# Rolling the thirty middle images of a four-layer kernel into a hardware loop of three images

## The chip, the cores and the metric

The kernel runs on one core of a Trainium2 chip. Its time is the device time of one execution, in microseconds (us). The kernel before takes 14134.04 us, the median of three runs (14127.32 to 14146.60). The profile comes from one execution, which took 14127.32 us; its recorded span is 14125.5 us, so 1.8 us lie outside the span.

The engines are TensorE (PE for matmuls, PEld for weight loads), VectorE (DVE), ScalarE (ACT), GpSimd (POOL), and SyncE (SP), which here issues all DMA transfers. Each engine has a sequencer that reads the engine's instructions in order. Some instructions are the sequencer's alone: a semaphore wait, a register operation, a branch. They are not counted as busy time of the engine. The profile marks the sequencer with a q (DVEq, POOLq).

## The reference: what is computed

Thirty-two images of 128 channels by 32x32 pixels pass four residual layers, each on a group-normalised input:

```python
x = x + _L0_conv_ref(_gn(x), ...)   # 3x3 convolution
x = x + _L1_conv_ref(_gn(x), ...)   # four-direction state-space scan over 1024 pixels
x = x + _L2_conv_ref(_gn(x), ...)   # gated row and column means, with two short scans
x = x + _L3_conv_ref(_gn(x), ...)   # four-qubit circuit per pixel
```

Layer 1 takes nearly all of the time. For each of 4 directions, 256 inner channels and 16 states it runs a recurrence over the 1024 pixels:

```python
dA = jnp.exp(dt_t[..., None] * A)
h = dA * h + (dt_t * u_t)[..., None] * B_t[:, None, :]
y = jnp.einsum('bdn,bn->bd', h, C_t)
```

## The kernel before

**Units.** A unit is one state n of one half (128) of the inner channels in one direction: 4 x 2 x 16 = 128 units per image, each a tile of 128 partitions by 1024 pixels. Per unit, four engines work in turn:

- ACT makes the decay exp(dt * A) (L1164) and raises `decay_ready`.
- The input dt * u * B is made in one of three ways, which the table `KINDS` chooses. In a D unit (70 per image) PE spreads the row B over the partitions into a PSUM slot (`spread_b`, raises `b_ready`), and DVE multiplies it in place by `du` (L1446, raises `input_ready`). In a P unit (52 per image) POOL multiplies `du` by a row that a DMA has broadcast (L954, raises `pool_input`). In a Z unit (6 per image) PE and ACT make it (`z_turned`).
- DVE runs the recurrence as one scan (L1460, raises `scan_done`).
- POOL multiplies the scans of two units by their C rows (L971, one 128x2048 product per pair, 64 per image, raises `prod_ready`), and PE adds the products up in PSUM (`y_acc`, L1487, raises `sum_done`).

The scans live in a ring of 8 unit buffers (`RING`), the C rows in 4 buffers, the broadcast B rows in 4.

**Side steps.** Everything else (layers 0, 2 and 3, the convolution and projections of layer 1, for this image and the next) is cut into small steps that a planner places between the units of each engine's program. Its result is a fixed order, the same for all middle images. `hold` writes the waits of a side step, `side` counts its completion.

**Semaphores and the image number.** No semaphore is ever reset. Every wait is for a count that has grown since the start of the program: unit u of image s waits for `scan_done >= s * UNITS + u + 1`, side steps for a base that grows by a fixed number per image (`bases`). In the DVE program a scan waits like this, in this order:

```python
dve.wait_ge(input_ready, s * N_D + number("D", u) + 1)
...
dve.wait_ge(decay_ready, s * UNITS + u + 1)
```

and a product on POOL like this:

```python
pool.wait_ge(c_in[k % CB_BUFS], 16 * (s * (PAIRS // CB_BUFS) + k // CB_BUFS) + 16)
pool.wait_ge(scan_done, s * UNITS + u + 1)
```

**The image loop.** `each_image` calls an engine's `image` function once per image at build time: "first", thirty times "mid", "last". So s is a plain number everywhere, every wait is for a constant, and each engine's program is one straight line of instructions for all 32 images.

An instruction carries one wait of its own. Where an operation waits for two semaphores, the builder puts one wait on the operation and the other on a separate wait instruction of the sequencer ahead of it. The profile calls that one EVENT_SEMAPHORE, and the chain of waits shows it as DVEq or POOLq.

Of the kernel before, what the change touches and what calls it, by code (L numbers as in the profile page):

```python
# [616 lines left out]
def four_layers(nc, images, x_in, keep, once, small, dtw, conv_wt, preb_row, qw, out):  # L617
# [36 lines left out]
    with ExitStack() as ctx:  # L654
# [91 lines left out]
        turns, turns_whole = q_sb[:, 48:96], scratch[0:1, 3408:3408 + 48]  # L746
# [34 lines left out]

        def each_image(eng, body):

            for s in range(images):
                body("first" if s == 0 else "last" if s == images - 1 else "mid", s)

        NONE = dict.fromkeys("PADG", 0)

# [27 lines left out]
        def _(sp):  # L816
# [48 lines left out]
            def image(kind, s):  # L865
# [26 lines left out]
                if kind != "last":  # L892
                    store_rows(0, base, of[("dt_cb_rows", 0, 1)])
                    for k in range(CB_BUFS):
                        load_pair(k, s + 1)

            each_image(sp, image)
            sp.wait_ge(*done(finish_base, finish_n[("result", 1)]))
            sp.dma_start(out[images - 1], x_old[:, :]).then_inc(out_stored, 16)
# [4 lines left out]
        def _(pool):  # L904
# [33 lines left out]
            def image(kind, s):  # L938
# [33 lines left out]
                side_steps(END["G"])  # L972

            each_image(pool, image)
            for _, name, e, _, after in finish:
                if e == "G":
# [5 lines left out]
        def _(act):  # L982
# [153 lines left out]
            def image(kind, s):  # L1136
# [34 lines left out]
                want(HOME)  # L1171

            each_image(act, image)
            for _, name, e, bank, after in finish:
                if e == "A":
# [619 lines left out]
```

## Time and profile before

| | |
|---|---|
| median of three runs | 14134.04 us |
| profiled execution, its span | 14127.32 us, 14125.5 us |
| instructions recorded | 172711 |
| POOL, DVE, PE, ACT busy share of the span | 94%, 92%, 89%, 74% |
| TensorE clock granted, mean of the run | 0.945 |
| DMA, mean | 222 GB/s |

The run is even. The 64 products of a middle image end about 433.5 us after those of the image before, all through the program, so one middle image stands for thirty. A busy share is an average; two engines above 90% that wait for each other leave the question open which of them sets the pace where. That is read from the waits and from the chain of waits, which follows the work that ended last back in time, at each step to what released it.

### The profile page before, as it was taken

Reading aid. Unit: us, or ns where it says so; the run is one execution under the profiler, and the core shown is the slowest. Engines: PE = TensorE matmul, PEld = TensorE weight load, DVE = VectorE, ACT = ScalarE, POOL = GpSimd, SP = SyncE. Lnnn points to the kernel's source line nnn. Section 1 sums busy time; section 2 is a strip of 40 time slices with the busy share of each in tenths; the row PEclk is TensorE's granted clock in tenths of the full one; section 3 lists DMA queues with packets and bytes.
Section 4 is the critical chain, followed back from the end, with each engine's and each line's share of the span. In section 5 each row is a group of like instructions: output and inputs, shape, how many; then the busy total and the mean of one; then the engine's idle time right before and its main releaser. Section 6 shows DMA issues by size and latency. Waiting matters only on the chain.

```text
span 14125.5 us, 172711 instructions
## 1 busy us (share of the span) xinstructions
PE 12502.9 (89%) x64412; PEld 8000.4 (57%) x64412; DVE 12955.6 (92%) x8813; ACT 10492.8 (74%) x14525; POOL 13337.0 (94%) x4106
## 2 busy tenths in 40 slices
PE   7889989899888898888988888988889989889886
PEld 4555555555555555555555555555555555555554
DVE  7999999999999999999999999999999999999986
ACT  5777777777777777777777777777777777777764
POOL 7999999999999999999999999999999999999985
PEclk8999999999999999999999999999999999999997
DMA  5665556655556655566555665555655556656653
GB/s 195 231 227 223 223 221 227 234 223 223 223 223 235 225 221 225 221 230 231 223 223 223 226 233 223 221 225 224 233 225 225 222 220 229 232 223 225 226 206 120
DMA packets 563751, 3131.63 MB, mean 222 GB/s; under 512 B 63826, under 2 KB 63834, under 8 KB 300642
## 3 DMA queue, kind: packets, MB, share of 16 engines
q1 hardware_dynamic: 562914, 3120.59, 58.6%
q8 instruction: 510, 8.36, 0.2%
q14 instruction: 327, 2.68, 0.1%
HBM read 3057.42 MB, written 46.14 MB: 220 GB/s over the span
## 4 chain that ended last, share of the span: by engine, by line
POOL 30%; issue 22%; PE 22%; DVE 20%; ACT 6%; POOLq 0%; DMA 0%; DVEq 0%; SPq 0%; ACTq 0%
POOL ring L971 20%; PE work L1472 12%; DVE ring L1460 11%; POOL ring L954 9%; DVE slot L1446 7%; PE y_acc L1487 6%; PE y_acc L1472 2%; PE slot L1472 2%; ACT L988 1%; ACT slot L1164 1%; ACT ring L1164 1%; ACT z_t L1067 1%; PE work L1487 1%; DVE du L1271 0%; PE slot L1487 0%
## 5 line engine op out<-in xcount | busy, mean ns | idle before, releaser
L971 POOL TENSOR_TENSOR ring<-ring,c_rows 128x2048 f32<-128x2048 f32 x2048 | 9284.2, 4540 | 435.6 <-DVE ring L1460 423.1
L1460 DVE TENSOR_TENSOR_SCAN ring<-ring,slot 128x1024 f32<-128x1024 f32 x2432 | 5544.3, 2284 | 162.5 <-PE slot L1487 68.4
L1487 PE MATMUL y_acc<-wk,ring 128*128 128x128 f32 x32768 | 4450.8, 284 | 515.1 <-POOL ring L971 447.4
L1487 PEld LDWEIGHTS y_acc<-wk,ring 128*128 128x128 f32 x32768 | 3941.3, 147 | 1565.5 <-POOL ring L971 671.3
L954 POOL TENSOR_TENSOR ring<-du,b_rows 128x1024 f32<-128x1024 f32 x1664 | 3938.4, 2368 | 63.3 <-DVE du L1271 54.2
L1460 DVE TENSOR_TENSOR_SCAN ring<-slot,ring 128x1024 f32<-128x1024 f32 x1664 | 3782.3, 2273 | 223.0 <-POOL ring L954 153.4
L1446 DVE TENSOR_TENSOR slot<-du,slot 128x1024 f32<-128x1024 f32 x2240 | 2713.8, 1212 | 138.4 <-PE slot L1472 134.2
L1164 ACT ACTIVATE slot<-dt,a_neg 128x1024 f32<-128x1024 f32 x1664 | 1854.2, 1114 | 1299.4 <-DVE ring L1460 1294.1
L1164 ACT ACTIVATE ring<-dt,a_neg 128x1024 f32<-128x1024 f32 x2432 | 2738.7, 1140 | 78.1 <-PE y_acc L1487 63.2
L1472 PE MATMUL work<-h_new,fused 128*128 128x512 f32 x4096 | 1935.9, 602 | 17.9 <-ACT yz L1076 8.8
L1472 PE MATMUL slot<-stack,sel 96*128 96x512 bf16 x4480 | 1407.4, 397 | 540.1 <-DVE ring L1460 503.9
L988 ACT ACT_TABLE_LOAD x1081 | 1386.9, 1283 | 19.1
L1472 PEld LDWEIGHTS slot<-stack,sel 96*128 96x128 bf16 x4480 | 343.3, 100 | 1491.1 <-DVE ring L1460 1038.2
L1472 PEld LDWEIGHTS work<-h_new,fused 128*128 128x128 f32 x4096 | 717.3, 190 | 740.4 <-issue 584.6
L1472 PE MATMUL work<-padded,wk 128*128 128x512 f32 (+1 forms) x1792 | 984.0, 652 | 55.8 <-ACT yz L1076 27.7
L1472 PE MATMUL work<-du,wk 128*128 128x512 f32 x1024 | 643.5, 715 | 76.2 <-ACT du L1055 73.8
L1047 ACT ACTIVATE du<-work,wk 128x512 f32<-128x512 f32 x512 | 350.1, 684 | 461.6 <-PE work L1472 459.4
L1472 PE MATMUL work<-stack,smallw 8*128 8x512 f32 x1024 | 577.3, 643 | 107.8 <-ACT u_conv L1027 71.5
L1038 ACT ACTIVATE stack<-work 32x512 bf16<-32x512 f32 x768 | 448.7, 584 | 285.4 <-PE work L1472 271.7
L1057 ACT ACTIVATE dt<-work 128x512 f32<-128x512 f32 x512 | 301.7, 589 | 374.1 <-PE work L1472 371.6
L1472 PEld LDWEIGHTS y_acc<-diag_d,u_conv 128*128 128x128 f32 x4096 | 524.6, 202 | 50.4 <-issue 22.8
L1472 PE MATMUL work<-u_conv,wk 128*128 128x512 f32 x1024 | 543.4, 656 | 8.9 <-ACT silu_z L1029 4.0
(182 smaller groups left out, 11296.9 us busy)
## 6 DMA issues: line engine op xcount, KB each, us to landing
c_rows<-cb_rows_scratch SPq DMA_DIRECT2D x2048, 1024.0 KB, 4.6
b_rows<-cb_rows_scratch SPq DMA_DIRECT2D x1664, 512.0 KB, 5.5
x_next<-in_x SPq DMA_DIRECT2D x32, 512.0 KB, 5.6
x_new_scratch<-x_next SPq DMA_DIRECT2D x32, 512.0 KB, 6.7
h_old<-h_new SPq DMA_DIRECT2D x32, 512.0 KB, 2.9
x_old<-x_new_scratch SPq DMA_DIRECT2D x32, 512.0 KB, 5.5
out<-x_old SPq DMA_DIRECT2D x32, 512.0 KB, 3.3
cb_rows_scratch<-stack SPq DMA_DIRECT2D x128, 96.0 KB
```

The costliest lines, as they stand in the source:

```text
L954: pool.tensor_tensor(ring[:, u % RING, :], du[:, h, :], b_rows[:, j % B_BUFS, :], ALU.mult).then_inc(pool_input, 1)
L971: pool.tensor_tensor(pair, pair, c_rows[:, k % CB_BUFS, :, :], ALU.mult).then_inc(prod_ready, 1)
L988: act.preload_act_table_set(name)
L1038: ins = act.activation(half(stack[r, d % 2, :], c), w[r, :], ACT.Copy)
L1047: ins = act.activation(half(du[:, h, :], c), w, ACT.Abs, bias=kc("dt_b", h, h + 1))
L1057: ins = act.activation(half(dt[:, name[2], :], name[3]), w, ACT.Copy)
L1067: ins = act.activation(z_t[:, j * P:(j + 1) * P], du_t[:, j * P:(j + 1) * P], ACT.Copy, scale=b_t[:, d % 2, j * NST + n:j * NST + n + 1])
L1164: act.activation(slot, dt[:, h, :], ACT.Exp, scale=a_neg[:, h * NST + n:h * NST + n + 1]).then_inc(decay_ready, 1)
L1446: dve.tensor_tensor(operand[u % 2], du[:, h, :], operand[u % 2], MUL).then_inc(input_ready, 1)
L1460: dve.tensor_tensor_scan(slot, a, b, 0.0, MUL, ADD).then_inc(scan_done, 1)
L1472: return pe.matmul(out_ap, w, x, start=start, stop=stop, skip_group_check=True)
L1487: ins = pe.matmul(chunk(out_t, j), chunk(x, j), kc("ident"), is_transpose=True, start=start and j % (BANK // P) == 0, stop=stop, skip_grou ...
```

## The change

The loop over the images becomes a hardware loop on each of the five engines. The first and the last image stay written out. The thirty middle ones become ten turns of a loop whose body holds three images:

```diff
         def each_image(eng, body):
-            for s in range(images):
-                body("first" if s == 0 else "last" if s == images - 1 else "mid", s)
+            body("first", 0)
+            if images > 2:
+                turns = next(k for k in (3, 2, 1) if (images - 2) % k == 0)
+                with eng.Fori(0, (images - 2) // turns) as t:
+                    for i in range(turns):
+                        body("mid", t * turns + 1 + i)
+            if images > 1:
+                body("last", images - 1)
```

In the loop the image number s is an expression of the loop's register t, so every count that a wait is for has to be computed into a register first. The data instructions and their order on each engine are the same as before. What is new in each engine's program: one branch into the loop, ten compare-and-branch instructions (nine of them taken, back to the start of the body), and register instructions ahead of the waits. The places of the waits move too. The built program shows it.

On DVE, from the D, P and D units near the start of a middle image, before (slot is the PSUM slot of the input, ring the scan's buffer; names in brackets are the semaphores waited for, and the last one is carried by the operation itself, the ones ahead of it by a wait instruction of the sequencer):

```order
L1446 TENSOR_TENSOR slot<-du,slot 128x1024 [waits b_ready]
L1460 SCALAR_TENSOR_TENSOR ring<-ring,slot 128x1024 [waits decay_ready,input_ready]
L1460 SCALAR_TENSOR_TENSOR ring<-slot,ring 128x1024 [waits decay_ready,pool_input]
L1446 TENSOR_TENSOR slot<-du,slot 128x1024 [waits b_ready]
L1460 SCALAR_TENSOR_TENSOR ring<-ring,slot 128x1024 [waits decay_ready,input_ready]
```

The same place in the loop's body now, on DVE (line numbers are 6 higher):

```order
L1451 REGISTER_ALU
L1452 TENSOR_TENSOR slot<-du,slot 128x1024 [waits b_ready]
L1463 REGISTER_ALU [waits input_ready]
L1466 SCALAR_TENSOR_TENSOR ring<-ring,slot 128x1024 [waits decay_ready]
L1461 REGISTER_ALU
L1463 REGISTER_ALU [waits pool_input]
L1466 SCALAR_TENSOR_TENSOR ring<-slot,ring 128x1024 [waits decay_ready]
L1451 REGISTER_ALU
L1452 TENSOR_TENSOR slot<-du,slot 128x1024 [waits b_ready]
L1463 REGISTER_ALU [waits input_ready]
L1466 SCALAR_TENSOR_TENSOR ring<-ring,slot 128x1024 [waits decay_ready]
```

The wait for DVE's own multiplication (`input_ready`) has moved from the scan to the register instruction ahead of it, which computes the count for `decay_ready`; the wait for ACT's decay has moved onto the scan. This holds for 70 scans of an image, and likewise for 52 scans with `pool_input` and 6 with `z_turned`.

On POOL, products (L971) and inputs (L954) near the start of a middle image, before:

```order
L971 TENSOR_TENSOR ring<-ring,c_rows 128x2048 [waits scan_done,c_in3]
L954 TENSOR_TENSOR ring<-du,b_rows 128x1024 [waits sum_done,b_in0]
L971 TENSOR_TENSOR ring<-ring,c_rows 128x2048 [waits scan_done,c_in0]
L954 TENSOR_TENSOR ring<-du,b_rows 128x1024 [waits sum_done,b_in1]
L971 TENSOR_TENSOR ring<-ring,c_rows 128x2048 [waits scan_done,c_in1]
```

```order
L975 REGISTER_ALU [waits c_in3]
L977 TENSOR_TENSOR ring<-ring,c_rows 128x2048 [waits scan_done]
L957 ISA
L960 TENSOR_TENSOR ring<-du,b_rows 128x1024 [waits sum_done,b_in0]
L974 ISA
L975 REGISTER_ALU [waits c_in0]
L977 TENSOR_TENSOR ring<-ring,c_rows 128x2048 [waits scan_done]
L960 TENSOR_TENSOR ring<-du,b_rows 128x1024 [waits sum_done,b_in1]
L975 REGISTER_ALU [waits c_in1]
L977 TENSOR_TENSOR ring<-ring,c_rows 128x2048 [waits scan_done]
```

The wait for the scan has moved the other way here: off a wait instruction of the sequencer and onto the product itself. The inputs keep their waits where they were.

The end of the loop's body on DVE, and the first operation of the last image behind it:

```order
L1463 REGISTER_ALU [waits pool_input]
L1466 SCALAR_TENSOR_TENSOR ring<-slot,ring 128x1024 [waits decay_ready]
L812 REGISTER_ALU
L1277 TENSOR_TENSOR du<-work,u_conv 128x512 [waits side_A]
L787 REGISTER_ALU
L787 COMPARE_AND_BRANCH
L1452 TENSOR_TENSOR slot<-du,slot 128x1024 [waits b_ready,side_D]
```

A turn of the loop thus ends with two instructions of the sequencer behind the last data instruction, and nothing there waits for another engine.

Counted in the built programs, the sequencer's own instructions per middle image (waits and register operations together) go from 141 to 339 on DVE, from 117 to 166 on POOL, from about 64 to 420 on ACT, from about 60 to 318 on PE, and from about 6 to 130 on SP.

## Rows read from the trace of the kernel before

**Rows 1.** The page: span, and busy time of each engine.
```profile
span 14125.5 us, 172711 instructions
PE 12502.9 (89%) x64412; PEld 8000.4 (57%) x64412; DVE 12955.6 (92%) x8813; ACT 10492.8 (74%) x14525; POOL 13337.0 (94%) x4106
```

**Rows 2.** Windows of one middle image each: stretch, length, busy us per engine (count).
```profile
5284.00:5718.00 434.00, 388.02 (x2012) 248.40 (x2012) 403.96 (x271) 328.05 (x454) 417.24 (x129) 0.95 0.60 226
5718.00:6151.00 433.00, 388.01 (x2012) 248.34 (x2012) 403.98 (x271) 328.04 (x454) 416.23 (x129) 0.95 0.60 225
```

**Rows 3.** Waits in the image 5284 to 5718, POOL's and DVE's: total us, times, longest.
```profile
POOL ring L971 <- DVE ring L1460: 12.7, 10, 2.2
...
DVE ring L1460 <- POOL ring L954: 3.9, 5, 1.1
DVE slot L1446 <- PE slot L1472: 3.7, 4, 2.5
DVE yz L1275 <- PE y_acc L1487: 3.3, 1, 3.3
...
DVE ring L1460 <- ACT ring L1164: 1.8, 2, 1.0
```

**Rows 4.** Chain of waits by line, image 5284 to 5718: shares of the stretch.
```profile
by line: issue 22.4%; POOL ring L971 21.9%; PE work L1472 11.3%; DVE ring L1460 10.9%; POOL ring L954 9.7%; DVE slot L1446 6.9%; PE y_acc L1487 5.9%; PE y_acc L1472 1.9%; PE slot L1472 1.6%; ACT slot L1164 0.7%; ACT L988 0.6%; ACT z_t L1067
```

**Rows 5.** The chain's pieces in two places: start us, us, what.
```profile
5305.78 1.22 DVE slot L1446
5307.00 0.02 issue
5307.02 1.77 DVE ring L1460
...
5423.47 2.30 DVE ring L1460
5425.76 0.02 issue
5425.79 0.02 POOLq L969
5425.80 0.08 issue
5425.89 0.02 POOLq L953
5425.90 4.53 POOL ring L971
```

**Rows 6.** Groups of instructions on DVE, whole run: busy, mean ns, idle before.
```profile
L1460 DVE TENSOR_TENSOR_SCAN ring<-ring,slot 128x1024 f32<-128x1024 f32 x2432 | 5544.3, 2284 | 162.5 <-PE slot L1487 68.4 <-ACT ring L1164 22.9 <-issue 0.2
L1446 DVE TENSOR_TENSOR slot<-du,slot 128x1024 f32<-128x1024 f32 x2240 | 2713.8, 1212 | 138.4 <-PE slot L1472 134.2
```

**Rows 7.** Timeline: a POOL operation released by DVE without a wait instruction.
```profile
5496.39 0.69 DVE L1314 TENSOR_REDUCE m<-work 128x32 f32<-128x512 f32 x1
...
5497.16 0.40 POOL L926 TENSOR_TENSOR m<-m,wk 128x128 f32<-128x128 f32 x1 [3.13 <-DVE m L1314]
```

**Rows 8.** Timeline of DVE across an image's end (start us, us, instruction, idle before).
```profile
5275.02 2.29 DVE L1460 TENSOR_TENSOR_SCAN ring<-ring,slot 128x1024 f32<-128x1024 f32 x1
5277.23 2.27 DVE L1460 TENSOR_TENSOR_SCAN ring<-slot,ring 128x1024 f32<-128x1024 f32 x1
5279.41 0.67 DVE L1271 TENSOR_TENSOR du<-work,u_conv 128x512 f32<-128x512 f32 x1
...
5286.99 1.22 DVE L1275 TENSOR_TENSOR yz<-y_acc,silu_z 128x1024 f32<-128x1024 f32 x1 [3.33 <-PE y_acc L1487]
```

**Rows 9.** Timeline of POOL at the same place.
```profile
5273.46 2.40 POOL L954 TENSOR_TENSOR ring<-du,b_rows 128x1024 f32<-128x1024 f32 x1
5275.80 9.03 POOL L971 TENSOR_TENSOR ring<-ring,c_rows 128x2048 f32<-128x2048 f32 x2
```

**Rows 10.** DMA issues on SP: count, KB each, median us to landing.
```profile
b_rows<-cb_rows_scratch SPq DMA_DIRECT2D x1664, 512.0 KB, 5.5
...
c_rows<-c_rows SPq DMA_DIRECT2D x4, 1.0 KB, 1.7
```

**Rows 11.** The longest wait of SP's sequencer, whole run.
```profile
SPq L855 <- POOL ring L971: 11188.8, 1920, 16.0
```

**Rows 12.** Timeline at the start: SP's sequencer issues a DMA.
```profile
3.70 0.33 SPq L824 DMA_DIRECT2D x_next<-in_x  x1
```

## Prediction, made before the changed kernel was run

> **What bounds the kernel now.** I read the page first. POOL is busy 13337.0 us of 14125.5 (94%), DVE 12955.6 (92%) [rows 1]. Neither share names a bound, so I took windows of one middle image each. POOL works 416 to 417 us and DVE 404 us in about 433.5 us [rows 2], so POOL has some 17 us left per image and DVE some 30. Then the waits inside one image. POOL waits for a scan of DVE 10 times, 12.7 us in all. DVE waits for POOL's inputs 5 times (3.9 us), for PE's spread rows 4 times (3.7 us), for PE's sum once (3.3 us) [rows 3]. The two engines take turns: in some stretches POOL runs without a gap and DVE waits, in others DVE does and POOL waits. The chain of waits says how much of an image stands on each: DVE's multiplication L1446 has 6.9% of the image's 434 us and the scans 10.9%, POOL's products 21.9% [rows 4]. The reader is to keep one number from there: 6.9% of 434 us is 29.9 us, and at 1.21 us each [rows 6] that is 25 of the 70 multiplications of an image that lie on the chain. Its pieces show what follows each: the scan of the same unit, on the same engine [rows 5].
>
> **The change, part by part.** No data instruction is added, dropped or moved. Three things are new: the places of the waits, the register instructions, and the branches.
>
> *A wait carried by an operation against one carried by the sequencer.* The trace of before has both for the same pair of engines. A product on POOL that waits for DVE has a sequencer instruction between: DVE's scan ends at 5423.47 + 2.30, and the product starts at 5425.90, with POOLq L969 in between [rows 5]: 0.13 to 0.14 us. The POOL operation L926 carries its wait for DVE itself: DVE ends at 5496.39 + 0.69 = 5497.08, POOL starts at 5497.16 [rows 7]: 0.08 us. So a wait held by the sequencer costs about 0.065 us more when it is the last to be met. When it has been met early, it costs nothing on a busy engine.
>
> *D scans on DVE: the loss.* Before, the multiplication's result was waited for by the scan itself. The multiplication ends at 5305.78 + 1.22 = 5307.00 and the scan starts at 5307.02 [rows 5]: 0.02 to 0.03 us. Now a register instruction waits for that result. It can't be met early, because DVE itself produces it: the sequencer stands until the multiplication is complete, then computes the count, then hands the scan over. This happens behind every one of the 70 multiplications of a middle image. Its price is the 0.065 us above, plus what a register operation takes beyond the wait instruction of before. The trace has no register operation. From below, the nearest row is the sequencer's own wait instruction, 0.02 us (POOLq L969, [rows 5]), so no more than before; from above the widest thing that a sequencer does here, the issue of a DMA, 0.33 us [rows 12]. I take 0.04 us more than the wait instruction, near the lower row, since both are short steps of the sequencer with no address work. That makes 0.11 us per D scan (bounds 0.065 and 0.065 + 0.31 = 0.375).
> On the chain: 25 x 0.11 = 2.75 us per image. The other 45 lie in stretches in which DVE waits for others afterwards, and its 30 us of idle time cover them. If that cover were gone, all 70 would count: 7.7 us.
>
> The Trainium skill (page "Advanced Engine Details and Errata", section "Sequencer and Instruction Queues") says that engine instructions are queued and wait there, while control instructions are executed by the sequencer in microcode, and others can be read and queued meanwhile. The trace agrees as far as it goes, with 0.08 against 0.14 us. Taken strictly, that others are queued while a control instruction executes, the rule would let the scan be queued beneath the standing register operation and take the 2.75 us away; the row in which POOLq L969 stands until the scan's end and the product follows it speaks against that.
>
> *Scans that wait for POOL or for PE and ACT (58 per image).* `pool_input` moves from the scan onto a register instruction. Met late 5 times per image [rows 3], so 5 x 0.11 = 0.55 us on DVE; the chain does not pass from L954 to a scan, so I count it at nothing, under cover of the 30 us. From below zero, from above 0.55.
>
> *Products on POOL and waits for decays: the gain.* The scan's completion is now waited for by the product itself, 0.065 us less each time it is late. That is 10 times per image [rows 3], 0.65 us; on the chain stand about 3 of them, 0.2 us. DVE's late waits for a decay get the same, 2 or 3 per image, 0.15 us. Together 0.35 us on the chain, at most 0.85.
>
> *The register instructions that wait for nothing.* DVE's sequencer gets 198 more instructions per image, ACT's 356, PE's 258, POOL's 49, SP's 124. Even at 0.1 us each the largest sum is 36 us of 433.5, on ACT, which is busy 328 [rows 2]. They run while the engine works on what is queued: 2.3 us per scan, 4.5 us per product. SP stands 11188.8 us in waits for products [rows 11]. So nothing, with 0 as the lower end, and as the upper end one 0.04 us step ahead of each of POOL's 14 or so late operations, 0.6 us.
>
> Net per middle image: 2.75 - 0.35 = 2.4 us, and 30 of them are 72 us.
>
> *The branches.* Nine are taken backwards on each engine. If the code at the target has to be fetched, the engine's queue covers some of it. At an image's end DVE has two scans and L1271 queued or running from 5275.02 to 5280.1, 5 us, of which its sequencer should be free of the last wait at about 5276, when POOL's input has come (5273.46 + 2.40, [rows 9]); and a later start is caught by the 3.33 us in which DVE waits for PE's sum a moment later [rows 8]. POOL has 9.03 us of products before it needs the next instruction [rows 9]. A fetch has no row here; by the nearest, a small DMA lands in 1.7 us and one of 512 KB in 5.5 [rows 10]. So between 0 and 5.5 us per turn; I take 1 us, nearer to covered, for what slips through: 9 us.
> The Trainium skill (page "Runtime: NRT & Kernel Launch", section "Instruction fetch mechanics") says that a taken branch to code outside the two fetched pages stalls until a DMA has brought the page, and that kernels therefore prefer full unrolling. It names no time; no run here shows it yet. Taken as uncovered, at 5.5 us, it would be the whole of rival 3.
>
> **Sum.** 72 + 9 = 81 us on the profiled execution's 14127.3 (span 14125.5 and 1.8 around it) gives 14208. That execution was the fastest of three and the median lies 6.7 us higher, so I forecast 14215 us, 0.6% slower. Its own range: with 0.065 per D scan and full gains of 0.85 it is +33 us, and with 0.15 per D scan and half of the covered scans exposed (47 in all) +210 us.
>
> **Rivals.**
> 1. *DVE's slack swallows it.* DVE is idle 30 us per image and would be later by 7.7. POOL is busier, and the ring lets DVE run units ahead of it. For: POOL needs 417 of 433.5. Against: POOL waits for scans 10 times in an image, so the slack isn't where the multiplications are. Time: some 10 us for the branches and the rest, 14145.
> 2. *Everything is exposed, or a register operation is long.* All 70 at 0.11 are 7.7 us, less 0.35, times 30 is 220 us, and 9 more: 14363. With 0.375 us for the 25 on the chain, 9.4 - 0.35 = 9.0 times 30 is 271 us: 14414. For: a delay on the chain makes others late. Against: DVE's waits for PE and POOL give some back.
> 3. *Only the branches cost.* The sequencer does not stand before the scan as I think, and the fetches are open: 9 x 5.5 = 50 us, 14184.
> 4. *Faster.* The place is POOL's product, from the moment its wait is its own: if the register operation hands the scan over as fast as the scan's own wait did, only the gains are left, 0.85 us x 30 = 26 us, less what the branches take: 14108 to 14117. It decides if the D scan's gap stays at about 0.03 us. Against it stands the 0.14 us of before.
> That the loop doesn't do what it says is no rival: the built program has the branches and the 339 sequencer instructions.
>
> **Chances.** A measurement here tells from no change what is beyond 0.2%, 28 us. Forecast 0.60 (of which 0.02 within 0.2%), rival 1 0.17, rival 2 0.11, rival 3 0.07 (of which 0.02 within), rival 4 0.05 (half of it beyond 0.2%, half within). Slower: 0.58 + 0.11 + 0.05, and 0.01 of rival 1, 0.75. Within: 0.02 + 0.16 + 0.02 + 0.02, 0.22. Faster: 0.03. The range of 8 in 10 leaves out most of rival 4, the low half of rival 1 and the longest of rival 2: 14138 to 14370.
>
> **What would show it.** In the changed kernel's profile: the gap from L1452 to L1466 on DVE is 0.13 us or more, where it was 0.02 to 0.03; POOL starts a late product 0.08 us after the scan, no longer 0.14; a middle image takes about 436 us; DVE's busy time per image is unchanged; every third image is longer by about 1 us, and its excess stands at the body's end. Wrong would make it: a gap that stays at 0.03 us (then rival 3 or 4), a gap that grows while the image stays at 433.5 (rival 1), an image of 441 us or more (rival 2), or a third image that is longer by over 5 us.

## The result, and the profile after

The changed kernel takes 14229.73 us, the median of four runs (14220.40 to 14238.92), against 14135.49 us for the kernel before in the same comparison: a ratio of 1.0070, 95% interval 1.0056 to 1.0085. That is 94 us slower. The forecast was 14215, its range 14138 to 14370. Three more runs of it took 14243.2 to 14245.5, so a difference of some 10 us from it means little. The profiled execution spans 14223.5 us, 98 more than that of before.

The page of the changed kernel, rows that answer to [rows 1], the chain by line, and the groups of [rows 6]; the first is busy time and its share:

```profile
PE 12521.2 (88%) x64412; PEld 7971.6 (56%) x64412; DVE 12957.9 (91%) x8813; ACT 10502.8 (74%) x14525; POOL 13343.7 (94%) x4106
...
POOL 46%; issue 33%; PE 9%; DVE 7%; ACT 3%; DMA 1%; POOLq 1%; DVEq 0%; SPq 0%; ACTq 0%
...
L977 POOL TENSOR_TENSOR ring<-ring,c_rows 128x2048 f32<-128x2048 f32 x2048 | 9290.7, 4543 | 481.7 <-DVE ring L1466 472.0
L1466 DVE TENSOR_TENSOR_SCAN ring<-ring,slot 128x1024 f32<-128x1024 f32 x2432 | 5544.8, 2284 | 327.5 <-PE slot L1493 58.2
...
L1452 DVE TENSOR_TENSOR slot<-du,slot 128x1024 f32<-128x1024 f32 x2240 | 2714.1, 1212 | 163.7 <-PE slot L1478 123.2
```

DVE and POOL are as busy as before to within 7 us. On these two engines all that has grown is idle time. Ahead of the scans whose input lies in a PSUM slot, 70 D and 6 Z per image, it is 327.5 us and was 162.5 [rows 6], ahead of their multiplications 163.7 and was 138.4, and POOL's products wait 472.0 us for scans, where they waited 423.1. Their instructions cost nothing more; waits do.

The row by engine is worth a second look. Before it was:

```profile
POOL 30%; issue 22%; PE 22%; DVE 20%; ACT 6%; POOLq 0%; DMA 0%; DVEq 0%; SPq 0%; ACTq 0%
```

The chain now has 46% on POOL and 7% on DVE, where it had 30% and 20%. From a multiplication to its scan it passes 7.2 times per middle image, before 24.9 times. The prediction's sum took the count of before; the section on why it was right comes back to this.

The chain of waits of the changed kernel behind a multiplication, to be set against [rows 5] (start us, us, what; of each piece the part that the chain counts):

```profile
1999.38 1.15 DVE slot L1452
2000.52 0.03 issue
2000.55 0.04 DVEq L1463
2000.59 0.04 issue
2000.63 0.07 DVE ring L1466
```

The multiplication ends at 2000.52. Then stands what was not there before: the sequencer's register instruction DVEq L1463, 0.04 us long, with 0.03 and 0.04 us of hand-over around it. The scan starts 0.11 us after the multiplication's end; in [rows 5] it was 0.02. Over all 2084 such neighbours in the trace the median gap is 122 ns, before 35 ns.

The timeline of DVE and of POOL where a product was late:

```profile
5553.35 2.28 DVE L1466 TENSOR_TENSOR_SCAN ring<-slot,ring 128x1024 f32<-128x1024 f32 x1
...
5555.71 4.53 POOL L977 TENSOR_TENSOR ring<-ring,c_rows 128x2048 f32<-128x2048 f32 x1 [1.91 <-DVE ring L1466]
```

The scan ends at 5555.63, POOL's product starts at 5555.71: 0.08 us, and no longer the 0.14 of [rows 5].

The length of an image, from the end of the 64th product of the image before to the end of its own, was 433.4 to 433.6 us for 24 of the 30 middle images before. Now it lies between 433.6 and 440.1, 436.6 in the mean. Windows of the changed kernel: three whole middle images, then two stretches near the start of a fourth (us, busy of the engines, PEclk, DMA):

```profile
4010.50:4444.30 433.80, 385.59 (x2012) 246.36 (x2012) 401.81 (x270) 325.21 (x452) 416.89 (x129) 0.96 0.60 225
8374.70:8814.60 439.90, 394.22 (x2012) 250.42 (x2012) 406.47 (x273) 331.50 (x457) 416.76 (x130) 0.94 0.60 223
8814.60:9249.90 435.30, 386.57 (x2012) 245.60 (x2012) 404.05 (x271) 328.45 (x454) 416.95 (x130) 0.96 0.61 225
1822.00:1832.00 10.00, 6.90 (x17) 3.55 (x16) 9.64 (x6) 4.28 (x5) 8.60 (x3) 0.50 0.48 175
1837.50:1840.50 3.00, 2.22 (x5) 0.59 (x4) 3.00 (x2) 2.12 (x3) 1.53 (x1) 1.00 0.21 45
```

Every middle image has the same instructions, yet one takes 433.8 and another 439.9 us, and PE is busy 8.6 us longer in the second, at a mean clock of 0.94 instead of 0.96. The last two rows show what that is: for ten microseconds of an image PE's granted clock is 0.50, the lower of its two levels (1.2 GHz), and a moment later 1.00 (2.4 GHz). In the kernel before, such stretches stand at the same places in image after image. Windows of it, each 16.6 us behind an image's start:

```profile
1400.00:1403.00 3.00, 3.00 (x13) 2.25 (x11) 2.31 (x3) 3.00 (x4) 3.00 (x2) 0.50 0.55 169
1833.50:1836.50 3.00, 3.00 (x12) 2.26 (x11) 2.36 (x3) 3.00 (x4) 3.00 (x2) 0.50 0.58 191
4001.00:4004.00 3.00, 3.00 (x13) 2.19 (x12) 2.24 (x3) 3.00 (x4) 3.00 (x2) 0.50 0.55 158
```

That regularity is what the prediction took for granted, and what the experiments are about.

### The profile page after: what moved, and what is told of

Read it like the earlier page. It is cut to its first block, busy times and chain, and to the rows that moved or that the text cites. A ratio compares the mean times of both kernels' runs of the same rounds, so it can differ in the third digit from the quotient of the medians.

```text
span 14223.5 us, 202410 instructions
## 1 busy us (share of the span) xinstructions
PE 12521.2 (88%) x64412; PEld 7971.6 (56%) x64412; DVE 12957.9 (91%) x8813; ACT 10502.8 (74%) x14525; POOL 13343.7 (94%) x4106
## 4 chain that ended last, share of the span: by engine, by line
POOL 46%; issue 33%; PE 9%; DVE 7%; ACT 3%; DMA 1%; POOLq 1%; DVEq 0%; SPq 0%; ACTq 0%
POOL ring L977 27%; POOL ring L960 17%; PE work L1478 5%; DVE ring L1466 4%; DVE slot L1452 2%; PE y_acc L1493 2%; ACT L994 1%; POOL yz L927 1%; PE slot L1478 1%; ACT ring L1170 1%; DMA b_rows<-cb_rows_scratch 1%; ACT u_conv L1033 0%; PE slot L1493 0%; PE y_acc L1478 0%; PE work L1493 0%
## 5 line engine op out<-in xcount | busy, mean ns | idle before, releaser
L977 POOL TENSOR_TENSOR ring<-ring,c_rows 128x2048 f32<-128x2048 f32 x2048 | 9290.7, 4543 | 481.7 <-DVE ring L1466 472.0
L1466 DVE TENSOR_TENSOR_SCAN ring<-ring,slot 128x1024 f32<-128x1024 f32 x2432 | 5544.8, 2284 | 327.5 <-PE slot L1493 58.2
L1452 DVE TENSOR_TENSOR slot<-du,slot 128x1024 f32<-128x1024 f32 x2240 | 2714.1, 1212 | 163.7 <-PE slot L1478 123.2
L1478 PE MATMUL work<-h_new,fused 128*128 128x512 f32 x4096 | 1977.9, 613 | 25.5 <-ACT yz L1082 19.3
L1073 ACT ACTIVATE z_t<-du_t,b_t 128x128 f32<-128x128 f32 x1536 | 490.4, 390 | 85.3 <-PE slot L1493 70.0
L1478 PEld LDWEIGHTS work<-padded,wk 128*128 128x128 f32 (+1 forms) x1792 | 311.4, 198 | 409.3 <-issue 232.2
```

Of the source, the lines that this page charges most:

```text
L977: pool.tensor_tensor(pair, pair, c_rows[:, k % CB_BUFS, :, :], ALU.mult).then_inc(prod_ready, 1)
L1073: ins = act.activation(z_t[:, j * P:(j + 1) * P], du_t[:, j * P:(j + 1) * P], ACT.Copy, scale=b_t[:, d % 2, j * NST + n:j * NST + n + 1])
L1452: dve.tensor_tensor(operand[u % 2], du[:, h, :], operand[u % 2], MUL).then_inc(input_ready, 1)
L1466: dve.tensor_tensor_scan(slot, a, b, 0.0, MUL, ADD).then_inc(scan_done, 1)
L1478: return pe.matmul(out_ap, w, x, start=start, stop=stop, skip_group_check=True)
```

## The experiments

All times are medians, over 5 or 11 runs (4 for the changed kernel); "change" is against the kernel before, timed with them. The mean middle image and the clock are the profiled execution's.

| kernel | us | change, 95% interval of the ratio | mean middle image | clock |
|---|---|---|---|---|
| before (profile of the start) | | | 433.3 | 0.945 |
| after | 14229.7 | +94, 1.0056 to 1.0085 | 436.6 | 0.946 |
| line_d_swap | 14206.6 | +67, 1.0035 to 1.0063 | 435.3 | 0.946 |
| line_pool_swap | 14208.0 | +68, 1.0032 to 1.0059 | 436.0 | 0.935 |
| line_all_swap | 14237.3 | +98, 1.0055 to 1.0082 | 437.1 | 0.940 |
| loop_d_back | 14198.3 | +59, 1.0022 to 1.0049 | 435.8 | 0.939 |
| loop_15 | 14238.0 | +98, 1.0060 to 1.0087 | 436.3 | 0.946 |
| line_pool_warm | 14136.5 | -1, 0.9989 to 1.0007 | 433.7 | 0.944 |
| before_warm | 14136.3 | -2, 0.9989 to 1.0007 | 433.8 | 0.944 |
| after_warm | 14242.5 | +105, 1.0060 to 1.0088 | 437.5 | 0.943 |
| loop_both_back | 14170.1 | +32, 1.0014 to 1.0032 | 435.2 | 0.939 |
| both_back_15 | 14136.9 | -2, 0.9990 to 1.0008 | 433.8 | 0.944 |
| both_back_1 | 14230.2 | +91, 1.0051 to 1.0078 | 437.0 | 0.936 |
| before_fill | 14115.7 | -23, 0.9976 to 0.9994 | 432.8 | 0.963 |

### The D scan's wait alone (line_d_swap)

The straight-line kernel; only for D units the two waits change places, so that the scan carries the decay's and a wait instruction stands for DVE's own multiplication.

```diff
                     if kind_of(u) == "D":
+                        dve.wait_ge(decay_ready, s * UNITS + u + 1)
                         dve.wait_ge(input_ready, s * N_D + number("D", u) + 1)
...
-                    dve.wait_ge(decay_ready, s * UNITS + u + 1)
+                    if kind_of(u) != "D":
+                        dve.wait_ge(decay_ready, s * UNITS + u + 1)
```

> The straight-line program of before, with one thing changed: in the 70 D scans of an image the wait for the decay is written ahead of the wait for the multiplication, so that the sequencer's wait instruction holds the wait for DVE's own multiplication and the scan holds the decay. No loop, no register operation, no branch. Theory A (the place of the wait sets the loss): the gap from L1446 to the D scan goes from 0.03 to about 0.10 us, 25 of them on the chain, so 1.65 us or a little more per image over 32 images: 14185 to 14205 us against 14135. Theory B (register operations load the sequencers): no register operations here, so within 14 us of 14135. Theory C (the nine branches and their code fetches make the loss): also 14135.

Measured: +67 us, without a loop, a register instruction or a branch. As a change it is what theory A gave (+50 to +70 us); the time, 14206.6, lies 2 us above its range, since the kernel before was 5 us slower in these runs. Theories B and C fail. Its chain of waits at one such place:

```profile
5317.93 1.14 DVE slot L1446
5319.07 0.03 issue
5319.09 0.02 DVEq L1450
5319.11 0.04 issue
5319.16 0.06 DVE ring L1462
```

The scan starts 0.09 us behind the multiplication; DVEq L1450 is the plain wait instruction, 0.02 us. The median gap is 103 ns, 68 more than before. The chain passes from a multiplication to its scan 29.9 times per middle image here, and 29.9 x 0.068 = 2.0 us is just what the mean image has grown (435.3 less 433.3). But single images do not show 2.0 us. Windows of three of them:

```profile
1395.60:1834.20 438.60, 392.60 (x2012) 251.51 (x2012) 403.85 (x271) 328.16 (x454) 416.63 (x129) 0.94 0.59 223
1834.20:2266.10 431.90, 380.87 (x2012) 241.95 (x2012) 403.96 (x271) 328.07 (x454) 416.76 (x130) 0.97 0.60 227
4007.30:4441.80 434.50, 387.67 (x2012) 248.23 (x2012) 403.71 (x271) 327.93 (x454) 416.68 (x130) 0.95 0.60 225
```

438.6, 431.9 and 434.5 us, though each has all seventy gaps; the one of 431.9 is quicker than any steady image of the kernel before, with a clock of 0.97. So PE's half-clock stretches decide more about a single image than the gaps do.

### The product's wait alone (line_pool_swap)

```diff
-                    pool.wait_ge(c_in[k % CB_BUFS], 16 * (s * (PAIRS // CB_BUFS) + k // CB_BUFS) + 16)
                     pool.wait_ge(scan_done, s * UNITS + u + 1)
+                    pool.wait_ge(c_in[k % CB_BUFS], 16 * (s * (PAIRS // CB_BUFS) + k // CB_BUFS) + 16)
```

> The straight-line program of before, with the two waits of a POOL product exchanged, so that the product itself waits for the scan and the sequencer's wait instruction for the C rows. Theory A: a late product starts 0.08 us behind the scan, no longer 0.14, 10 times per image and 3 of them on the chain: 0.2 to 0.65 us per image, so 14115 to 14129 us against 14135, possibly too little to tell. Theories B and C say nothing of it: 14135.

Measured: +68 us. Every theory failed: products that start 0.066 us sooner make the kernel slower. The image lengths name the reason. But for two near the end they are not spread but fall on two values, 433.3 to 433.5 us (as before) and 436.4 to 437.2. Windows of this kernel: the first microseconds of a long image and of a short one, then the two images whole.

```profile
1392.30:1395.30 3.00, 2.96 (x14) 2.97 (x15) 0.00 (x0) 0.00 (x0) 3.00 (x2) 0.51 1.02 407
4013.70:4016.70 3.00, 2.90 (x20) 2.46 (x21) 0.80 (x1) 0.00 (x0) 3.00 (x3) 1.00 0.96 366
1392.30:1829.20 436.90, 392.71 (x2012) 252.04 (x2012) 404.13 (x271) 328.08 (x454) 416.68 (x129) 0.94 0.60 224
4013.70:4447.20 433.50, 387.44 (x2012) 248.11 (x2012) 403.96 (x271) 328.09 (x454) 416.84 (x130) 0.95 0.60 226
```

Both stretches begin with the same work, the sixteen y_acc matmuls of the last product. Ahead of both PE had stood idle for 2.5 us, waiting for that product of POOL. In the first, PE's granted clock is 0.51 in the mean, from the first matmul on, in the second 1.00. The timeline of DVE shows the consequence, its wait for the sum (L1275, answering to [rows 8]):

```profile
1395.84 1.23 DVE L1275 TENSOR_TENSOR yz<-y_acc,silu_z 128x1024 f32<-128x1024 f32 x1 [4.69 <-PE y_acc L1487]
...
4015.91 1.23 DVE L1275 TENSOR_TENSOR yz<-y_acc,silu_z 128x1024 f32<-128x1024 f32 x1 [3.27 <-PE y_acc L1487]
```

4.69 us of waiting against 3.27: the image starts 1.4 us late, and more half-clock stretches follow in places where the short image has none. At the 28th product the short image is 0.3 us ahead of the kernel before and the long one 3.3 us behind. Over all middle images, 19 of the 22 long ones have a clock of 0.50 or 0.51 in their first 3 us, and of the six short ones one does. So this start goes with nearly all long images, but it isn't all there is to them.

From this came theory L: the chip lowers PE's clock behind idle stretches, but not behind each of them; the steady kernel before has its idle stretches where the drops do least harm, and a shift of nanoseconds is enough to move one to a place where it hurts. That the places before are the harmless ones is a guess so far; before_fill tests it below. The Trainium skill (page "TensorE: Matmul & The Clock Gate", section "What's actually happening") says that the clock is switched between 1.2 and 2.4 GHz after recent activity, on a raster that runs freely and isn't tied to the kernel. By that rule, the same idle time could lower the clock in one image and not in the next; the two rows above agree.

### Kept busy through the last wait (line_pool_warm, before_warm, after_warm)

Eight matmuls of zeros, added to y_acc, fill PE's wait for the last product of each image. They change no result.

```diff
+                    if u == UNITS - 2:
+                        for j in range(8):
+                            mm(half(y_acc, j % 2), zero[:, :], zero[:, 0:1].broadcast_to([P, BANK]), False, False)
                     pe.wait_ge(prod_ready, s * PAIRS + u // 2 + 1)
```

> The kernel before with the product's wait for the scan placed on the product (as in the first such run, 14208 us, +68), and with the eight matmuls of zeros ahead of TensorE's wait for the last product of each image. Theory L: the half-clock stretch at the image's end that this kernel shows in most of its images (y_acc's sixteen matmuls at 0.213 us instead of 0.109 us apart, DVE's next operation 1.4 us late, a further stretch soon after) no longer begins: nearly all images take 433.5 us again, 14125 to 14155 us. Theory A: the product's earlier start costs by itself or through a wait not yet named: 14190 to 14215 us, the matmuls change nothing.

> The kernel before, with eight matmuls of zeros (512 columns each, added to y_acc) on TensorE ahead of its wait for the last product of each image, where it stands idle for 2.5 us. They change no result. Theory L (the lost time of the experiments is TensorE at half clock in the first microseconds of an image, after that idle stretch): the kernel before has no half-clock stretch at the image's end, so nothing is to be had: 14125 to 14150 us. Theory A (the loss is a sum of longer gaps on the chain of waits, the clock plays no part): also 14125 to 14150. This run is the control for the two others with these matmuls; outside of that range they have a cost of their own, at most 8 x 0.43 - 2.5 = 0.9 us per image at half clock, 30 us in all.

> The changed kernel with the eight matmuls of zeros at the same place. Its images have different lengths, 433.6 to 440.1 us, and about a third of them a half-clock stretch at their end or in their first 11 us. Theory L: those go, up to 3.4 us for ten to fifteen images: 14180 to 14215 us; what remains over 14140 is the longer gap ahead of DVE's scans of D units. Theory A (the sum of gaps and branches): unchanged, 14220 to 14240 us.

Measured: line_pool_warm -1 us, before_warm -2, after_warm +105. The whole 68 us of the product's wait are gone, and the control shows that the matmuls themselves give and take nothing. All thirty middle images of line_pool_warm now begin at a clock of 1.00. So that loss came from PE's clock at the image's end, and the product's placement has no price of its own. The timeline of PE in line_pool_warm at an image's end:

```profile
1817.23 1.97 PE L1489 MATMUL y_acc<-wk,ring 128*128 128x128 f32 x16 [1.24 <-POOL ring L973]
1819.03 1.90 PE L1474 MATMUL y_acc<-zero 128*128 128x512 bf16 x8
1821.72 1.96 PE L1489 MATMUL y_acc<-wk,ring 128*128 128x128 f32 x16 [0.79 <-POOL ring L973]
```

The idle stretch ahead of the last sum is 0.79 us, no longer 2.5. In the changed kernel, though, the same matmuls help nothing, and there theory L's forecast (14180 to 14215) failed; theory A's (14220 to 14240) was missed by 2 us. All images of after_warm begin at full clock too, but they have half-clock stretches elsewhere, for instance from 15 to 22 and from 199 to 220 us of the image, and those are not reached.

### The D scans' waits put back, and fewer branches, in the loop (loop_d_back, loop_15)

loop_d_back computes the decay's count ahead of the multiplication, for D units only, so that the scan carries its input's wait again.

```diff
+                        count = s * UNITS + u + 1
+                        isinstance(count, int) or dve.to_reg(count)
                         dve.wait_ge(b_ready, s * N_D + number("D", u) + 1)
...
-                    dve.wait_ge(decay_ready, s * UNITS + u + 1)
+                    dve.wait_ge(decay_ready, count if kind_of(u) == "D" else s * UNITS + u + 1)
```

loop_15 has 15 images in the body and one taken branch in place of nine.

```diff
-                turns = next(k for k in (3, 2, 1) if (images - 2) % k == 0)
+                turns = 15
```

> The looped kernel with the count for the decay of a D scan computed ahead of the multiplication, so that the scan itself waits for the multiplication again; the nine branches, the code fetches and nearly all register operations stay. Theory A: the gap of a D scan is back at 0.03 us and some 2.6 us per image are gone; what is left are the branches (about 10 to 15 us in all) less the gain on POOL: 14130 to 14155 us. Theory B: about as many register operations, so 14215 to 14235. Theory C: the branches stay, so 14215 to 14235.

> The looped kernel with 15 images in the body and two turns: one taken branch per engine where there were nine; waits and register operations per image as in the looped kernel. Theory A: eight branches less at 1 to 2 us each, 14212 to 14222 us against 14230. Theory C: nearly all of the loss of 94 us goes, 14140 to 14150. Theory B: 14230.

Measured: loop_d_back 14198.3 us (14174.8 to 14218.3), which gives back only some 32 us, and lies in no theory's range (A 14130 to 14155, B and C 14215 to 14235); its median gap is 35 ns again. loop_15 took 14238.0 (14218.0 to 14268.5), no gain to be seen from eight branches fewer, and theory C failed. Taken one by one from the changed kernel, neither part is worth what it seems to be by the sum.

### Both waits put back in the loop, with 9, 1 and 29 taken branches

loop_both_back, against the changed kernel, for every product on POOL and for units of all three kinds on DVE:

```diff
+                    count = s * UNITS + u + 1
+                    isinstance(count, int) or pool.to_reg(count)
                     pool.wait_ge(c_in[k % CB_BUFS], 16 * (s * (PAIRS // CB_BUFS) + k // CB_BUFS) + 16)
-                    pool.wait_ge(scan_done, s * UNITS + u + 1)
+                    pool.wait_ge(scan_done, count)
...
                     side_steps(2 * u)
+                    count = s * UNITS + u + 1
+                    isinstance(count, int) or dve.to_reg(count)
...
-                    dve.wait_ge(decay_ready, s * UNITS + u + 1)
+                    dve.wait_ge(decay_ready, count)
```

both_back_15 and both_back_1 are the same with 15 images and with 1 image in the body.

> The changed kernel, its loop and all its branches kept, with both waits back where they stand in the straight program: the count for the later wait is computed ahead of the earlier one, so that DVE's scans of all three kinds wait for their input and POOL's products for their c rows on the operation, the other wait on a wait instruction. Theory P (the placement of the waits is the whole loss): 14130 to 14155 us, all images at 433.5 us. Theory R (register instructions and the refetch of code behind a branch shift things by enough to throw the kernel out of its pattern whatever the waits): 14170 to 14205 us, as the run with only the D scans' waits put back (14198).

> The hardware loop with both waits back (14170 us with three images in the body and nine taken branches), now with fifteen images in the body and one taken branch. Theory B (the 32 us that were left are the first image behind each taken branch, 437.1 instead of 433.4 us in the trace: TensorE stands 5 us for its code, and a half-clock stretch at 6.2 us of the image follows): one such image is left, 14135 to 14150 us. Theory R (the register instructions hold the rest): 14160 to 14185 us.

> The same with one image in the body and twenty-nine taken branches. Theory B: 29 x 3.6 = 104 us over 14138, 14225 to 14260 us. Theory R: the number of branches does not matter, 14160 to 14185 us.

Measured: +32, -2 and +91 us. The 14170.1 us of loop_both_back lie at the lower end of theory R's range; the two other runs then decide against theory R, and for the branches. All register instructions are in each of the three, 203740 instructions in both_back_15 against 172711 before, and with one taken branch the loop costs nothing that the interval (0.9990 to 1.0008) would show. So the register instructions are free to within 0.1%, and once the waits stand as before, what is left goes with the number of taken branches. PE's waits in loop_both_back that end on nothing but its own instruction stream:

```profile
PE slot L1482 <- issue: 29.7, 9, 3.5
```

Nine, one for each taken branch. In both_back_15 it is one, and in both_back_1 the page of waits has 27 of PE and 29 of DVE:

```profile
PE slot L1482 <- issue: 3.3, 1, 3.3
```

```profile
DVE slot L1456 <- issue: 102.5, 29, 4.1
...
PE slot L1482 <- issue: 91.8, 27, 6.1
```

The timeline of PE across one of the nine in loop_both_back, then windows of it: the image behind that branch and the next one, and the same stretch of both, 6.3 us behind their start:

```profile
8348.73 1.97 PE L1497 MATMUL y_acc<-wk,ring 128*128 128x128 f32 x16 [2.50 <-POOL ring L979]
8353.95 0.60 PE L1482 MATMUL slot<-stack,sel 96*128 96x512 bf16 x2 [3.25 <-issue]
8354.39 7.01 PE L1482 MATMUL work<-h_new,fused 128*128 128x512 f32 x12
```

```profile
8348.70:8785.70 437.00, 390.06 (x2012) 249.06 (x2012) 406.56 (x273) 330.75 (x457) 416.84 (x129) 0.95 0.59 223
8785.70:9219.10 433.40, 388.80 (x2012) 248.69 (x2012) 404.05 (x271) 327.94 (x454) 416.71 (x129) 0.95 0.61 226
8355.00:8358.00 3.00, 3.00 (x4) 1.09 (x4) 2.97 (x3) 2.19 (x2) 2.65 (x1) 0.50 0.59 175
8792.00:8795.00 3.00, 1.55 (x5) 0.39 (x4) 2.96 (x3) 1.51 (x2) 3.00 (x1) 1.00 0.04 16
```

PE stands 3.25 us with its sums done and its next spread not there. It isn't the only engine that stands. The waits of DVE in the same run, then the timelines of DVE and of ACT across this branch, and DVE's first operation of the next image that needs the sum:

```profile
DVE slot L1456 <- issue: 33.2, 9, 4.1
```

```profile
8347.70 1.23 DVE L1456 TENSOR_TENSOR slot<-du,slot 128x1024 f32<-128x1024 f32 x1 [3.75 <-issue]
8349.61 2.29 DVE L1470 TENSOR_TENSOR_SCAN ring<-ring,slot 128x1024 f32<-128x1024 f32 x1 [0.67 <-ACT ring L1172]
8351.81 1.20 DVE L1283 TENSOR_TENSOR yz<-y_acc,silu_z 128x1024 f32<-128x1024 f32 x1
...
8348.35 1.15 ACT L1172 ACTIVATE ring<-dt,a_neg 128x1024 f32<-128x1024 f32 x1 [5.13 <-issue]
...
8787.86 1.23 DVE L1283 TENSOR_TENSOR yz<-y_acc,silu_z 128x1024 f32<-128x1024 f32 x1 [3.20 <-PE y_acc L1497]
```

DVE stands 3.75 us for its next multiplication, ACT 5.13 us for its next decay, and DVE's scan then waits another 0.67 us for that decay. In the next image DVE waits 3.20 us for PE's sum at this place (L1283); behind the branch it doesn't wait there at all. So that wait takes up most of the stall, and the first product ends 0.85 to 1.2 us later behind the nine branches. That is the direct part. The rest comes later in the image: PE's clock is 0.50 where the next image has 1.00, and the image takes 437.0 in place of 433.4 us. Over the nine, the mean is 437.0, and nine times 3.6 is 32 us, as much as was measured. The sum isn't as clean as that: six of the other 21 images of this execution are long too, 435.9 to 437.1 us, and it took 14181.8 us, 12 more than the median of its kernel. How much of the 3.6 us is the late start, and how much the clock, was not tested. With one image in the body DVE stands 3.5 us and PE 3.4 us a time; +91 us are 3.1 per branch, at the low end of what theory B gave (14225 to 14260).

### All waits as in the changed kernel, in a straight line (line_all_swap)

The edits of line_d_swap and line_pool_swap together, and the same for DVE's scans of P and Z units.

> The straight-line kernel, no loop and no register instruction, with every wait of DVE's scans and of POOL's products placed as in the changed kernel. The two swaps alone cost 67 us (DVE) and 68 us (POOL). Theory L (POOL's 68 us are half-clock stretches behind TensorE's wait at the image's end; DVE's longer gap puts the images at other points, so that POOL's part need not return): 14190 to 14225 us, clearly less than the sum. Theory A (each placement has a price of its own): 14140 + 67 + 68 = 14275, 14255 to 14295 us.

Measured: 14237.3 us, +98. That is the changed kernel's time (14229.7, single runs up to 14245.5), with no loop. It lies between the two forecasts (L 14190 to 14225, A 14255 to 14295), and it is clearly not 67 + 68. So the placement of the waits alone is enough for a loss of this size, and given it, nine branches add nothing that can be seen, in line with loop_15. Single runs of these kernels lie up to 50 us apart, so a small cost of the branches could hide there.

### PE's idle stretches filled in the kernel before (before_fill)

```diff
+FILL_ADD = {18: 2, 22: 2, 24: 2, 26: 1, 28: 2, 46: 1, 50: 4, 76: 4, 78: 2, 82: 6, 92: 1, 124: 5, 126: 8}
+FILL_SPREAD = {0: 5, 11: 2, 13: 2, 18: 5, 27: 3, 30: 2, 49: 4, 61: 2, 63: 5, 69: 5, 111: 2, 123: 2}
```

The numbers are matmuls of zeros ahead of a unit's sum and of a spread; eight more stand ahead of one dt projection, and ahead of the first filled spread PE has one wait more per image (both not shown).

> The kernel before with some 75 matmuls of zeros per image (512 columns each, added to y_acc while it is open) in twenty-five of TensorE's idle stretches, each filled by less than it lasts, so that the half-clock stretches that follow them (8 per image, 41 us at half clock) get fewer. Theory L' (half-clock stretches on the way to DVE's and POOL's waits cost time in the kernel before as well): some of them go, 430 to 432.5 us per image, 14030 to 14110 us. Theory N (those that stand in the kernel before lie where nobody waits): 14125 to 14160 us. Beyond 14160 the matmuls get in the way.

Measured: 14115.7 us, faster than the kernel before by 0.15% (interval 0.06 to 0.24%) and than the changed one by 0.8%. It lies between the ranges of theory L' (14030 to 14110) and theory N (14125 to 14160). Windows of two images:

```profile
7009.00:7442.70 433.70, 399.89 (x2094) 249.48 (x2094) 404.38 (x271) 327.65 (x454) 416.64 (x130) 0.97 0.60 225
7875.60:8305.80 430.20, 394.77 (x2094) 247.60 (x2094) 404.09 (x271) 328.16 (x454) 416.70 (x130) 0.98 0.61 226
```

The clock rises to 0.97 and 0.98, yet most images stay at 433.6 us; six of thirty take 429.7 to 430.2. Some of the half-clock time of the kernel before does stand on the way, but most of what these matmuls remove did not.

## Why the prediction was right, and where it was not

**The time and the side: right.** 14229.7 against 14215, in the forecast's own range.

**The D scan's gap: right in mechanism, its price somewhat high.** 0.11 us more was forecast, 0.087 came (122 less 35 ns): 0.068 for the wait's place, by the straight-line kernel, and some 0.02 for the register instruction, which is 0.04 us long where the wait instruction has 0.02. The sign "0.13 us or more" was missed by 8 ns. At line_d_swap's gap the prediction's count gives 25 x 0.068 x 30 = 51 us and that run's own count 61; 67 were measured.

**The 25 multiplications on the chain: not borne out in the changed kernel.** Its own chain has 7.2 per middle image, line_all_swap's with the same waits 24.9, line_d_swap's 29.9. DVE and POOL are nearly equally loaded (91% and 94%), and the chain can run over either. A count taken before the change says little about the chain after it, and 7.2 x 0.087 x 30 would be 19 us.

**The gain on POOL's products: wrong, sign included.** The wait did get 0.065 us shorter, as said. But the gain of "0.35 us on the chain" became a loss of 68 us when the product's wait was moved alone. The step that failed is the unspoken one under the whole sum: that every other duration stays as it was. PE's does not: line_pool_swap and line_pool_warm differ by the filled idle stretch alone, and by 72 us.

**The register instructions that wait for nothing: right.** 31029 more instructions in both_back_15 cost nothing measurable.

**The branches: wrong twice, in opposite ways.** With the waits back in place, nine cost 32 us, not 9. The forecast had DVE's queued work cover its fetch; it doesn't, DVE stands 3.7 us in the mean behind each of the nine. What covers it is the 3.33 us wait for PE's sum that the forecast named second, and the 0.85 to 1.2 us by which the first product is late are near the 1 us it took. POOL's cover held, 3.3 us of such waits in all nine. The forecast did not look at ACT and PE, which stand 5.1 and 3.3 us, and it had no term for PE's clock behind such a stop. In the changed kernel the branches cost nothing more that can be seen on top of the waits (line_all_swap, loop_15). Its nine images behind a taken branch take 438.1 us in the mean, the other 21 436.0, which would fit the sign "every third image longer". But every third image of line_all_swap, which has no loop, differs as much (436.7, 438.3 and 436.2 us for the three thirds), so this doesn't show it. That line_all_swap comes to the same time without branches stays unexplained but for the observation that the prices do not add: 67, 68 and 32 would be 167, and 94 were measured.

**What stays open.** How the 94 us divide between gaps on the chain and half-clock stretches. By the gaps alone, 25 to 29.9 x 0.087 x 30 are 65 to 78 us, and by the changed kernel's own chain 19. The granted clock of each image says a little more. Time at half clock is here the image's length times 2 x (1 - its mean granted clock); all numbers are from the thirty middle images of one profiled execution each:

| kernel | at half clock per middle image, mean | its images with about 41 us of it (as a steady image before) take | correlation of length and half-clock time |
|---|---|---|---|
| before | 40.3 us | 433.1 to 433.6 us | 0.84 |
| line_pool_swap | 50.0 | 433.3 to 433.5 | 0.87 |
| line_d_swap | 38.8 | 434.5 to 436.9 | 0.96 |
| after | 40.0 | 435.2 to 437.4 | 0.90 |

line_pool_swap loses only where it has more half-clock time. The two kernels with the longer gap have no more of it than before, and are longer at the same amount. So their loss isn't more time at half clock; it is the gaps, or the places where the stretches now stand, and no run parts the two. Four images of the changed kernel take 433.6 to 433.9 us with every gap in them, with 27 to 34 us at half clock. That the forecast came within 15 us owes something to luck: an overrated gap, a count that the changed kernel's chain doesn't show, a gain that wasn't, and a clock that it had not counted nearly cancel.

**The rivals.** Rival 1, slack swallows the gap, is refuted in the mean by line_d_swap, though the slack does swallow it in single images. Rival 2 needed images of 441 us or more; the mean is 436.6 and the longest 440.1. Rival 3 had the branches at up to 50 us; with the waits back they are 32. Rival 4 is refuted by the gap in the chain.

## What to carry to other kernels

When a tuned kernel runs in a strictly repeating pattern and PE has waits of some microseconds in it, look at the granted clock of the same stretch in several repeats before summing nanoseconds: if the half-clock stretches stand at fixed places, any small shift, also a gain, can cost more than itself. In a hardware loop, compute the count of the later wait ahead of the earlier one, so that an engine's wait for its own last result stays on the operation, and put enough work into the body that taken branches are few: here the loop then cost nothing measurable. Measure an edit in the company it will have, since such prices do not add. And when two engines are nearly equally loaded, don't count on the chain of before to be the chain of after.

## What the runs showed of the hardware

- On DVE, a wait for the engine's own last result costs 35 ns on the operation, 103 ns on a wait instruction, and 122 ns on a register instruction (medians of the gap from the multiplication to the scan).
- Behind a taken branch the engines stand: in loop_both_back DVE 3.7 us, ACT 5.1 us and PE 3.3 us in the mean of nine; POOL, with 9 us of products in hand, 0.4 us. The Trainium skill (page "Runtime: NRT & Kernel Launch", section "Instruction fetch mechanics") says that such a branch stalls for a fetch of the target's code; the nine waits each of PE and DVE agree, and one taken branch in place of nine leaves one of each.
- The same 2.5 us of idle time on PE was followed by matmuls at the full clock in one image and at half in another, within one execution.
- Image lengths cluster: 433.5 and 436.9 us in line_pool_swap, 433.6 and 429.8 in before_fill. In the short image of line_pool_swap shown above the 4th to the 31st product come 0.25 to 0.4 us sooner than before, and the image still takes 433.5 us: a gain of that size is not passed on.
